# A graph network on one core: first step reordered, the old edge state turned on the way in, gathers in fours

## The reference

```python
edge = swish(edge_attr_raw @ enc_W + enc_b)              # 50000 x 4 -> 50000 x 128
for _ in range(4):
    e_in = concatenate([edge, x[src], x[dst]], axis=-1)  # 50000 x 384
    edge = edge + layernorm(swish(e_in @ eW1 + eb1) @ eW2 + eb2, eg, ebeta)
    agg = segment_sum(edge, dst, 3125)
    n_in = concatenate([x, agg], axis=-1)
    x = x + layernorm(swish(n_in @ nW1 + nb1) @ nW2 + nb2, ng, nbeta)
return layernorm(x0 + x)
```

## Time and profile before

| what | value |
|---|---|
| median of the runs | 3197.7 us (3197.43 to 3201.09, 3 runs) |
| the profiled execution | 3224.33 us, span 3222.6 us |
| mean granted TensorE clock | 0.947 |
| PE matmul busy | 2595.9 us, 81% |
| DVE busy | 2090.2 us, 65% |
| ACT busy | 1869.0 us, 58% |
| POOL busy | 1518.2 us, 47% |
| DMA | 512.86 MB, mean 159 GB/s |
| first window matmul (L1594) of the four steps | 93.02, 1022.55, 1758.31, 2494.33 us |

### The profile page before, as it was taken

The page is one execution under the profiler, slowest core; times in us unless marked ns, Lnnn a source line. Parts: engine busy times, 40 slices in busy tenths (PEclk is TensorE's granted clock), DMA queues, the critical chain, the costliest instruction groups (busy, mean ns, idle before and its releaser), DMA issues.

```text
span 3222.6 us, 82752 instructions
## 1 busy us (share of the span) xinstructions
PE 2595.9 (81%) x27702; PEld 1937.5 (60%) x27702; DVE 2090.2 (65%) x6292; ACT 1869.0 (58%) x5337; POOL 1518.2 (47%) x1581
## 2 busy tenths in 40 slices
PE   3778888888896888888887788888887788888886
PEld 1456666666673666666674566666664566666665
DVE  5566667777774566666674466666675466666667
ACT  2556566666653666666663566666664466666664
POOL 0544454544412555555521555555530655555540
PEclk9888888899898999999999999999999899999998
DMA  3544444444425788777744677787754666666650
GB/s 105 154 131 140 135 134 141 142 142 142 142 85 139 184 200 202 204 202 207 203 138 139 168 205 204 198 205 203 204 156 124 152 166 160 164 159 164 165 135 21
DMA packets 649002, 512.86 MB, mean 159 GB/s; under 512 B 363436, under 2 KB 560178, under 8 KB 648568
## 3 DMA queue, kind: packets, MB, share of 16 engines
q1 hardware_dynamic: 573304, 301.83, 36.6%
q0 software_dynamic: 75264, 205.62, 22.2%
HBM read 312.28 MB, written 117.85 MB: 133 GB/s over the span
## 4 chain that ended last, share of the span: by engine, by line
PE 73%; issue 14%; DVE 8%; ACT 1%; DMA 1%; another core or an unknown queue 1%; DVEq 1%; POOL 1%; ACTq 0%; SPq 0%; POOLq 0%
PE psum L1632 19%; PE psum L1613 14%; PE psum L1602 12%; PE psum L1663 7%; PE psum L1644 6%; PE psum L1594 5%; PE psum L1382 3%; PE psum L2040 2%; DVE arena L1851 2%; PE psum L2079 2%; PE psum L2053 1%; DVE arena L1825 1%; PE psum L1659 1%; DVE arena L1862 1%
## 5 line engine op out<-in xcount | busy, mean ns | idle before, releaser
L1571 POOL DMA_INDIRECT arena<-node_tables,idx_all x1568 | 1515.6, 967 | 1606.6 <-remote 555.1
L1815 DVE SCALAR_TENSOR_TENSOR arena<-psum,arena 128x1024 f16<-128x1024 f32 x392 | 479.2, 1223 | 666.8 <-issue 571.6
L1726 ACT ACTIVATE arena<-psum 128x1024 f16<-128x1024 f32 x392 | 401.5, 1024 | 848.0 <-PE psum L1613 460.6
L1632 PE MATMUL psum<-w_hi,arena 128*128 128x128 f16 x6272 | 675.2, 225 | 130.4 <-issue 122.4
L1632 PEld LDWEIGHTS psum<-w_hi,arena 128*128 128x128 f16 x6272 | 516.0, 101 | 262.5 <-issue 218.2
L1602 PE MATMUL psum<-ident,arena 128*128 128x128 f16 x6272 | 507.2, 222 | 166.9 <-issue 148.1
L1632 PE MATMUL psum<-w_lo,arena 128*128 128x128 f16 x3136 | 591.2, 225 | 40.3 <-issue 37.4
L1602 PEld LDWEIGHTS psum<-ident,arena 128*128 128x128 f16 x6272 | 402.3, 99 | 248.9 <-issue 217.1
L1749 ACT ACTIVATE arena<-psum 128x128 f32<-128x128 f32 x1568 | 412.8, 278 | 199.7 <-remote 160.0
L1851 DVE SCALAR_TENSOR_TENSOR arena<-arena,psum 128x128 f32<-128x128 f32 x1568 | 482.3, 340 | 6.1 <-remote 2.6
L1613 PE MATMUL psum<-arena,w_hi 128*128 128x512 f16 x1568 | 481.7, 389 | 5.5 <-issue 5.5
(11 more groups left out here) (169 smaller groups left out, 2730.7 us busy)
## 6 DMA issues: line engine op xcount, KB each, us to landing
state<-arena SPq DMA_DIRECT2D x294, 256.0 KB
arena<-node_tables SPq DMA_DIRECT2D x784, 64.0 KB
arena<-matrices SPq DMA_DIRECT2D x294, 128.0 KB
node_tables<-arena SPq DMA_DIRECT2D x100, 256.0 KB, 2.2
arena<-node_tables,idx_all POOLq DMA_INDIRECT x1568
arena<-rel_rows SPq DMA_DIRECT2D x98, 128.0 KB
matrices<-arena SPq DMA_DIRECT2D x98, 128.0 KB
arena<-state SPq DMA_TRANSPOSE x294
```

Source lines behind the costliest of these rows:

```text
L1571: pool.indirect_dma_start(out=rows[n % R][:, t, :], out_offset=None, in_=p_table, in_offset=bass.IndirectOffsetOnAxis(ap=idx_all[:, n % G1 ...
L1632: x = pe.matmul(ps_v(k2)[:, t * P:(t + 1) * P], h[k2][:, half, t * P:(t + 1) * P], w[:, half, :], start=False, stop=half == 1 and h is hl, ...
L1726: act.activation(hh[k2], ps_h(k2), ACT.Silu).then_inc(S("hh"), 1)
L1815: dve.scalar_tensor_tensor(hl[k2], ps_h(k2), 1.0, hh[k2], ALU.mult, ALU.subtract).then_inc(S("hl"), 1)
```

## The change

The change has these parts:

- HOLD becomes TPG. The third gather of a group no longer waits, so four gathers are issued behind each other.
- In steps 1 to 3 the old state is loaded without a transpose, edge-major, into `st_in`. PE transposes the tiles of group n + 1 behind `hidden(n)` (`turn`, 8 transposes into the f16 bank `ps_t`), ACT copies that bank to `eT` (`turned`, 128x1024) behind `silu(n)`, and L1613 reads `eT`. The 8 matmuls of `turn_back` are gone there. `scale` reads the low part of the old state from `st_in` in SBUF and not from PSUM, and a new DVE operation `add_old` (128x512) adds the high part. The load waits for `new`, no longer for `turned`.
- In steps 1 to 3 the bias eb2 comes from a PE matmul (L1627, 128x512) at the head of `output`, and ACT's `seed` is left to step 0.
- In step 0, PE's `encode(n + 2)` goes from behind `hidden` to the end of the iteration, and ACT's `encode_silu`, `seed` and `encode_high` go behind `squares` and `high`.
- In all steps DVE's `add_window` goes to the start of the slot and takes the group one older; the operations of `root` are grouped anew. Each step has one more slot at its end, behind the node update's second chunk.

```diff
--- before.py
+++ after.py
@@ -45,8 +45,7 @@
 R = 4
 R8 = 8
 RE = 8
-HOLD = 2
-BIAS_ACT = True
+HOLD = TPG
 R12 = 12
 LAG = 4
 EARLY = 4
@@ -1335,6 +1334,9 @@
             def newton_base(self, n):
                 return n // 2 * NEWTON_OPS
 
+            def loaded(self, n):
+                return self.S(f"st{n % RE}"), 16 * (self.ring(n, RE) - self.before(n % RE, RE))
+
             def before(self, k, r):
 
                 return len(range(k, G1, r))
@@ -1507,10 +1509,9 @@
                     sp.dma_start(matrices[n, :, :], both[n % R12]).then_inc(S(f"oh{n % R}"), 16)
 
                 def load_state(n):
-                    sp.wait_ge(S("turned"), n - RE + 1)
+                    sp.wait_ge(S("turned") if n - RE < G1 else S("new"), n - RE + 1)
                     sp.wait_ge(S(f"out{(n - G1) % R}"), 16 * self.ring(n - G1))
-                    sp.dma_start(turned_in[n % RE].rearrange("f k (t e) -> f (k t) e", t=TPG),
-                                 state[n % G1, :, :], transpose=True).then_inc(S(f"st{n % RE}"), 16)
+                    sp.dma_start(st_in[n % RE].rearrange("p k e -> p (k e)"), state[n % G1, :, :]).then_inc(S(f"st{n % RE}"), 16)
 
                 def load_matrices(n):
                     sp.wait_ge(S("h"), n - R + 1)
@@ -1604,21 +1605,35 @@
                                               start=False, stop=False, skip_group_check=True)
                     x.then_inc(S("src"), 1)
                     if s:
-                        pe.wait_ge(S(f"st{n % RE}"), 16 * (self.ring(n, RE) - self.before(n % RE, RE)))
+                        pe.wait_ge(S("eT"), n - G1 + 1)
                     else:
                         pe.wait_ge(Z("lo"), n + 1)
+                    old = eT[k2] if s else turned_in[n % RE]
                     for half in range(2):
                         cols = slice(half * D, (half + 1) * D)
                         for w, p in ((w1_hi, 0), (w1_hi, 1), (w1_lo, 0)):
-                            x = pe.matmul(ps_h(k2)[:, half, :], w[:, cols], turned_in[n % RE][:, p, :],
+                            x = pe.matmul(ps_h(k2)[:, half, :], w[:, cols], old[:, p, :],
                                           start=False, stop=w is w1_lo, skip_group_check=True)
                     x.then_inc(S("h"), 1)
 
+                def turn(n):
+
+                    if not first <= n <= last or s == 0:
+                        return
+                    pe.wait_ge(*self.loaded(n))
+                    if n > G1:
+                        pe.wait_ge(S("eT"), n - G1)
+                    for p in range(2):
+                        for t in range(TPG):
+                            m = p * TPG + t
+                            x = pe.transpose(ps_t[:, m * P:(m + 1) * P], st_in[n % RE][:, p, t * P:(t + 1) * P], ident16[:, :])
+                    x.then_inc(S("transposed"), 1)
+
                 def output(n):
 
                     k2 = n % 2
-                    if BIAS_ACT and n - first >= 2:
-                        pe.wait_ge(S("seed"), n - 2 * s - 1)
+                    if s == 0 and n >= 2:
+                        pe.wait_ge(S("seed"), n - 1)
                     else:
                         if n >= 2:
                             pe.wait_ge(S("gu"), n - 1)
@@ -1635,7 +1650,7 @@
 
                 def turn_back(n):
 
-                    if n < first:
+                    if n < first or s:
                         return
                     if n:
                         pe.wait_ge(S("new"), n)
@@ -1676,13 +1691,15 @@
                     pe.wait_ge(ND("plo"), NT * s)
                 else:
                     pe.wait_ge(Z("tab_lo"), NT)
+                turn(first)
                 for n in range(first, last + 1):
                     hidden(n)
-                    encode(n + 2)
+                    turn(n + 1)
                     if n > first:
                         output(n - 1)
                     turn_back(n - LAG)
                     node_sums(n - LAG - 3)
+                    encode(n + 2)
                 output(last)
                 turn_back(last - 3)
                 node_sums(last - 6)
@@ -1728,11 +1745,10 @@
 
                 def seed(n):
 
-                    if not BIAS_ACT or n - first < 2:
+                    if s or n < 2:
                         return
                     act.wait_ge(S("gu"), n - 1)
-                    if s == 0:
-                        act.wait_ge(Z("enc"), min(n + 3, G1))
+                    act.wait_ge(Z("enc"), min(n + 3, G1))
                     act.copy(ps_v(n % 2).rearrange("p (t f) -> p t f", t=TPG),
                              v_row[:, :].unsqueeze(1).to_broadcast([P, TPG, D])).then_inc(S("seed"), 1)
 
@@ -1763,15 +1779,27 @@
                     act.copy(st_out[k][:, 0, :], e_new[k]).then_inc(S("eh"), 1)
 
                 node_hidden, node_output, node_tables_of, normalise = node.act_parts(act, s)
+                def turned(n):
+
+                    if not first <= n <= last or s == 0:
+                        return
+                    act.wait_ge(S("transposed"), n - G1 + 1)
+                    if n - 2 >= G1:
+                        act.wait_ge(S("h"), n - 1)
+                    act.copy(eT[n % 2], ps_t[:, :].rearrange("c (k e) -> c k e", k=2)).then_inc(S("eT"), 1)
+
                 encode_silu, encode_high = self.encode_acts(act) if s == 0 else (nothing, nothing)
+                turned(first)
                 for n in range(first, last + 1):
                     silu(n)
-                    encode_silu(n + 2)
-                    seed(n)
+                    turned(n + 1)
                     if n > first:
                         squares(n - 1)
                     high(n - LAG - 1)
-                    encode_high(n + 2)
+                    if s == 0:
+                        encode_silu(n + 2)
+                        seed(n)
+                        encode_high(n + 2)
                 squares(last)
                 high(last - 4)
                 node_hidden(0)
@@ -1845,13 +1873,27 @@
                     if t == 0:
                         dve.wait_ge(S("newton"), self.newton_base(n) + NEWTON_OPS)
                         dve.wait_ge(S("gu"), n + 1)
-                        dve.wait_ge(S("turned"), n + 1)
+                        if s:
+                            dve.wait_ge(*self.loaded(n))
+                        else:
+                            dve.wait_ge(S("turned"), n + 1)
                         if n >= R:
                             dve.wait_ge(S("el"), n - R + 1)
-                    x = dve.scalar_tensor_tensor(e_new[k][:, t * P:(t + 1) * P], gu[k][:, t * P:(t + 1) * P],
-                                                 rs[pair][:, m:m + 1], ps_e[:, t * P:(t + 1) * P], ALU.mult, ALU.add)
-                    if t == TPG - 1:
+                    cols = slice(t * P, (t + 1) * P)
+                    old = st_in[n % RE][:, 1, cols] if s else ps_e[:, cols]
+                    x = dve.scalar_tensor_tensor(e_new[k][:, cols], gu[k][:, cols], rs[pair][:, m:m + 1], old, ALU.mult, ALU.add)
+                    if t == TPG - 1 and s:
+                        x.then_inc(S("scaled"), 1)
+                    elif t == TPG - 1:
                         x.then_inc(S("new"), 1)
+
+                def add_old(n):
+
+                    if not here(n) or s == 0:
+                        return
+                    dve.wait_ge(S("scaled"), n - G1 + 1)
+                    dve.scalar_tensor_tensor(e_new[n % R], e_new[n % R], 1.0, st_in[n % RE][:, 0, :],
+                                             ALU.mult, ALU.add).then_inc(S("new"), 1)
 
                 def low_new(n):
 
@@ -1892,28 +1934,27 @@
                 matrices_of, first_low = self.first_matrices(dve) if s == 0 else (nothing, nothing)
 
                 def slot(n):
-                    w = window(n - LAG - 3)
+                    add_window(n - LAG - 4, window(n - LAG - 4))
                     matrices_of(n + 2)
                     first_low(n + 1)
                     low(n)
                     if n % 2:
-                        root(n - 3, 0, 1)
-                        add_window(n - LAG - 3, w)
-                        root(n - 3, 1, 2)
+                        root(n - 3, 0, 2)
                         for t in range(TPG):
                             root(n - 3, t + 2, t + 3)
                             scale(n - LAG, t)
                         root(n - 3, 6, 7)
+                        add_old(n - LAG)
+                        root(n - 3, 7, 8)
                         low_new(n - LAG - 2)
-                        root(n - 3, 7, 9)
+                        root(n - 3, 8, 9)
                         gains(n - 1)
                     else:
-                        root(n - 4, 9, 10)
-                        add_window(n - LAG - 3, w)
-                        root(n - 4, 10, NEWTON_OPS)
+                        root(n - 4, 9, NEWTON_OPS)
                         low_new(n - LAG - 2)
                         for t in range(TPG):
```

(3 more changed lines are left out.)

## The result

The changed kernel takes 3122.85 us (median of 4 runs, 3121.84 to 3124.14) against 3197.56 of before (4 runs, 3188.35 to 3201.09): ratio 0.977, 95% interval 0.975 to 0.979. That is 75 us faster where 150 were forecast: the sign was right, the size half. Its profiled execution took 3122.29 us, 102 less than the profiled one of before (3224.33), which lay 27 us above the median of its kernel while this one lies at its own.

A forecast was written before the change was run, and what follows sets the result against it. PE was followed, held by a wait ring with DVE in step 0 and mutually with GpSimd's gathers later. Step 0 -140, later steps -22, ends +12: -150 us from 3197.7, rounded 3050; range 2900 to 3220.

The forecast's parts named there:

- The ring of step 0: Step 0: DVE's window sum and PE's encoding wait on each other; reordering cuts 8.61 to 7.1 us a group, -140 us.
- the 6.6 of the earlier trace: Start of step 0: two iterations in 13.2 us, 6.6 each, read as PE's period next to four gathers in a row.
- the half microsecond that I added for the late chain: Step 0: 7.1 us taken, half a microsecond over early rows, which have little of the late chain (no sums, no window).
- four gathers without a pause: GpSimd's gathers, four with one pause of 1.5 after them: cycle 6.2 us, alone a gain of 0.3 a group.
- the gathers' cycle of 6.2 us: Later steps: four gathers 4.7 us plus pause 1.5, the lower bound of the period; 6.45 taken, -22 us.
- Rival A: Steps 1 to 3: burst of four holds PE longer than two pairs, 7.45 us a group, +254; total 3384; chance 0.20.
- 4.1 us become 5.1, hidden: Later steps: ACT loses the seed, gains a 128x1024 copy of 1.02 us; its work a group stays hidden.
- The plain load: Later steps: without transposing loads, queues look like step 0's, so 6.6 rather than 7.23 us a group holds.
- The ends of the steps: Step ends: later window sum 2 us x 4, turn and copy ahead of first groups 1.5 x 3: +12, bounds 0 and 30.
- The base: Profiled execution 3224.3 us, 27 above the runs' median; difference taken to hold, so -150 was set against 3197.7.
- Rival B: Later steps: hold goes with the transposes, GpSimd's pause shrinks, cycle 5.75 us, -215; total 2845; chance 0.15.
- Rival C: Step 0 keeps a ring through other waits, period 7.8 us, -75; total 3124; chance 0.18.

The follow-up runs named there:

- the third experiment: One series, kernel before 3190.63: load of before with HOLD = 2 3011.80, with HOLD = TPG 3169.43 us; plain load 3015.39 and 3128.64, all with step 0 reordered.
- experiment 1: Against kernel before (2709.44 us): step 0 reordering alone 2590.80, HOLD = TPG alone 2700.59; changed kernel with HOLD = 2 2650.92.
- with holds: Series in which PE is often halted in later steps and GpSimd pauses; kernel before took 3190.6 and 3234.5 us in two, 3197.56 in the first pair.
- Without holds: Four series in which PE is seldom halted in later steps and GpSimd goes on almost without a pause; kernel before took 2696 to 2728 us.
- experiment 5: Changed kernel, unchanged, timed against kernel before (2696.33 us): 2648.28, ratio 0.982; also step 0 reordering with eight gathers in a row: 2594.59.

## Why the prediction was half right

**The ring of step 0: right.** The step 0 part is worth 179 us with pairs of gathers. 7.1 us a group was forecast for the changed kernel, 7.22 measured (7.14 in the third experiment): -124 us against -140, first groups included. But I had taken the 6.6 of the earlier trace rows as what PE reaches beside bursts, and so the bursts as free. The second of those two iterations in fact ran beside a pair: its gathers start at 139.90 and 141.15 us, the third only at 143.08. 6.6 is what step 0 reaches with pairs; with fours it is 7.15. That 7.1 came close is luck in part: the half microsecond that I added for the late chain was the squares' wait. PE's work in step 0 is 6.24, not 6.1. And I counted nothing for a clock that rises in step 0. It did rise, from 0.89 to 1.00 (and from 0.95 to 1.00 in experiment 1); how much of the gain is the clock's and how much the ring's, no run tells.

**The step that failed is "four gathers without a pause".** I took the gathers' cycle of 6.2 us as the floor of the later steps, a gain of 0.3 from its shortening, and let PE's smaller work of 5.08 make up some of the hold: 6.45. What the runs show in its place is that the run of four costs: 113 us in all with the plain load, 158 with the load of before, where I had counted on a gain. The cycle bounded nothing. In the changed kernel a run lasts 4.8 us, and then GpSimd waits for PE's `src` signal, 1.6 us in the mean in the later steps and 2.2 in step 0: the pause follows PE and doesn't lead it. In the later steps the chain is PE and its own halts, 1.07 us a group. The loop there took 6.57 instead of 6.45: +11 us where -22 was forecast. Rival A's mechanism, a burst that holds PE's work back longer than two pairs do, is what happened, at less than half of its price: HOLD = TPG adds 0.26 us a group with the plain load (6.34 to 6.61) and 0.39 with the load of before (6.42 to 6.81), where I had put 0.92. It doesn't turn the sign, as step 0 pays for it.

**What was left out of the sum** is the late signal to ACT. I had priced ACT's work ("4.1 us become 5.1, hidden") and not its waits, though the delay was to be seen in the trace of before, where the squares of step 1 start 2.7 us after the output's last matmul. In step 0 that wait is on the chain and takes the period from 6.6 to 7.2; in the later steps it is not.

**The plain load: right in direction where bursts are long.** From the load of before to the plain one, with turn, bias and `add_old` in the bundle: +4 us with HOLD = 2, -41 with HOLD = TPG, one run each. The share of the DMA engines falls from 0.79 at 205 GB/s to 0.70 at 209 with holds, and from 1.12 at 248 to 0.81 at 245 without (the share as printed; it can exceed 1). So the Trainium skill's rule that transposing DMAs are as fast as regular ones ("Advanced Engine Details and Errata", X-Bar Transpose) is not borne out by these shares, and yet it comes near for the time where the pairs stand. What the new path adds to PE, DVE and ACT didn't lengthen the period with holds (6.34 against 6.42). It wasn't hidden under the gathers' cycle, though: PE loses 6.42 - 4.86 = 1.56 us a group beyond its work with the load of before and 6.34 - 5.08 = 1.26 with the plain one, which pays for the 0.22 of the bias. Without holds the new path costs 60 us against the step 0 part, in the longer gathers of experiment 5.

**The ends of the steps:** +12 forecast. The first twelve groups of steps 1 to 3 cost 2 to 3 us more each, the tails 0 to 3 each, and the last groups ahead of the tails gave back 3: +11.

**The base.** I carried the difference over to the median. Of the shortfall of 75 us, 27 are that the profiled execution of before lay that much above its median and the one of after did not, 16 step 0, and 33 the later loop. Rival B fell: the pause grew instead of shrinking. Rival C, another ring in step 0, came about by its own sign, a new wait of 1 us or more a group, which is ACT's 2 us at the squares; but the period with it is 7.2 and not 7.8.

**The better version.** The step 0 part alone (HOLD = 2, the rest as before) takes 3011.80 where before takes 3190.63 and the changed kernel 3128.64, and 0.957 of before against 0.982 in series without holds. It is ahead of both kernels in either condition. With holds it has one run, without them eight in two series.

## What to carry to other kernels

When an engine that runs bursts delays the signals of another, price what waits for those signals, not only the engine that is halted: look for the consumer whose work plus wait makes the period, here ACT in step 0 with 5.1 + 2. Then read the chain stretch by stretch before you believe it: ACT's 14% of the whole span lay for the most part in the loop of step 0 (58% of its 592 us), and the same wait in the later steps made no period. A pause that looks like lost time on a side engine can be what lets signals through, so test it by itself before it is taken out. And set sums against the median, asking of each profile where its own excess lies: here 27 of 75 us were the base.

## What the chip showed that was not expected

The kernel before took 2696 to 2728 us in four series and 3190 to 3235 in three, the first pair's among them. In the longer ones PE is halted near each run of gathers (in step 1 of before most halts end 2.9 us after the start of a pair that lasts 2.2), and in the later steps ACT's squares start 2.6 us (pairs) to 3.1 us (fours) after the output's last matmul, in the median; in the others it is 1.3 us with before's order (1.0 with the changed one), and in the later steps GpSimd pauses in few groups or none. The mean granted clock is lower by 0.02 in the longer ones (0.947 against 0.966 for the kernel before, 0.970 against 0.986 for the changed one), too little for times that are 18% longer. The chip alone doesn't set it: the record names chip 1 for the series at 2709 us and again for the one at 3234, 16 minutes later. What does, no run tells. A change whose worth hangs on such waits is worth different amounts: the changed kernel has ratios of 0.977, 0.981, 0.995 and 0.982 to before, and HOLD = TPG costs 113 to 158 us in one series and nothing in another.
